# Perceiver layer on one core: a 320-byte gap in front of the transposed token rows in SBUF

## The reference, cut to what matters

```python
x = x + cross_attention(layernorm(x), ctx_2048)   # 4096 context rows + the 256 new ones, one head of 512
x = x + latent_attention(layernorm(x))            # 16 heads, low-rank queries, keys and values, causal, rotary
x = x + moe(layernorm(x))                         # 32 experts, 8 per token in 4 of 8 groups, and a shared expert
```

## Time and profile before

| | us |
|---|---|
| device time, median of 3 runs (lowest, highest) | 524.89 (524.79, 531.13) |
| device time of the profiled execution | 523.41 |
| its span | 521.4 |
| TensorE matmuls, busy in the span | 510.9 (98%) |
| TensorE weight loads | 458.6 (88%) |
| VectorE | 389.1 (75%) |
| ScalarE | 304.4 (58%) |
| GpSimd | 29.4 (6%) |

### The profile page before, as it was taken

The page is one execution under the profiler, slowest core; times in us unless marked ns, Lnnn a source line. Parts: engine busy times, 40 slices in busy tenths (PEclk is TensorE's granted clock), DMA queues, the critical chain, the costliest instruction groups (busy, mean ns, idle before and its releaser), DMA issues.

```text
span 521.4 us, 9657 instructions
## 1 busy us (share of the span) xinstructions
PE 510.9 (98%) x3454; PEld 458.6 (88%) x3454; DVE 389.1 (75%) x616; ACT 304.4 (58%) x470; POOL 29.4 (6%) x48
## 2 busy tenths in 40 slices
PE   8999999999999999989999999999999999999997
PEld 7988888888777998969899999999999999999997
DVE  6777555557889888867787777677776877778675
ACT  5665586655367776664664655546565465645631
POOL 1000000000524113001000000000000000000000
PEclk9999999999999999999999999999999999999999
DMA  8775634545412233333545464655656555464521
GB/s 290 295 232 174 198 123 132 167 162 158 152 35 77 77 97 145 121 123 137 203 142 194 171 224 155 224 182 180 210 163 229 163 200 201 165 233 152 215 72 40
DMA packets 19459, 86.24 MB, mean 165 GB/s; under 512 B 2160, under 2 KB 2416, under 8 KB 19312
## 3 DMA queue, kind: packets, MB, share of 16 engines
q1 hardware_dynamic: 19440, 85.99, 49.0%
HBM read 85.46 MB, written 0.52 MB: 165 GB/s over the span
## 4 chain that ended last, share of the span: by engine, by line
PE 90%; DVE 5%; ACT 2%; issue 1%; DMA 1%; SPq 0%; ACTq 0%; DVEq 0%
PE bank L936 31%; PE bank L429 17%; PE bank L433 16%; PE bank L432 16%; PE bank L437 2%; PE bank L438 1%; PE bank L439 1%; PE bank L573 1%; DVE w_lo L282 1%; PE bank L715 1%; DMA raw<-wq_dram 1%; PE bank L735 1%; PE bank L696 1%; ACT operands L305 1%; DVE xt_lo L330 1%
## 5 line engine op out<-in xcount | busy, mean ns | idle before, releaser
L277 ACT CAST w_hi<-raw 128x768 fp32r<-128x768 f32 (+3 forms) x158 | 159.0, 1041 | 96.6 <-PE bank L936 82.6
L282 DVE TENSOR_TENSOR w_lo<-raw,w_hi 128x1280 fp32r<-128x1280 f32 (+3 forms) x156 | 182.8, 1213 | 13.8 <-ACT w_hi L277 11.7
L429 PE MATMUL bank<-w_hi,operands 128*128 128x512 f32 (+1 forms) x322 | 125.8, 391 | 1.6 <-DVE operands L330 1.0
L433 PE MATMUL bank<-w_hi,operands 128*128 128x512 f32 (+1 forms) x322 | 124.5, 387 | 0.0
L432 PE MATMUL bank<-w_lo,operands 128*128 128x512 f32 (+1 forms) x322 | 123.8, 385 | 0.0
L936 PE MATMUL bank<-xt_hi,w_lo 128*128 128x256 f32 x512 | 105.3, 277 | 0.0
L936 PE MATMUL bank<-xt_hi,w_hi 128*128 128x256 f32 x512 | 105.3, 277 | 0.0
L936 PE MATMUL bank<-xt_lo,w_hi 128*128 128x256 f32 x512 | 105.1, 277 | 0.0
L936 PEld LDWEIGHTS bank<-xt_hi,w_hi 128*128 128x128 f32 x512 | 81.8, 188 | 2.6
L936 PEld LDWEIGHTS bank<-xt_lo,w_hi 128*128 128x128 f32 x512 | 79.8, 188 | 0.0
L936 PEld LDWEIGHTS bank<-xt_hi,w_lo 128*128 128x128 f32 x512 | 79.7, 188 | 0.0
(11 more groups left out here) (182 smaller groups left out, 563.2 us busy)
## 6 DMA issues: line engine op xcount, KB each, us to landing
raw<-w_exp_dram SPq DMA_DIRECT2D x34, 896.0 KB, 4.7
raw<-w_exp_dram SPq DMA_DIRECT2D x34, 640.0 KB, 5.6
raw<-ctx_t_dram SPq DMA_DIRECT2D x16, 512.0 KB, 4.7
raw<-ctx_n_dram SPq DMA_DIRECT2D x16, 512.0 KB, 4.2
raw<-w_mla_dram SPq DMA_DIRECT2D x8, 512.0 KB, 3.5
raw<-w_mla_dram SPq DMA_DIRECT2D x8, 448.0 KB, 3.8
raw<-wq_dram SPq DMA_DIRECT2D x4, 256.0 KB, 5.2
raw<-wk_dram SPq DMA_DIRECT2D x2, 512.0 KB, 7.1
```

What stands on the lines that cost most here:

```text
L277: act.copy(w_hi[:, t.slot, at:at + n], raw[:, t.slot, at:at + n]).then_inc(hi_split[k], 1)
L282: eng.tensor_tensor(w_lo[:, t.slot, at:at + n], raw[:, t.slot, at:at + n], w_hi[:, t.slot, at:at + n].bitcast(F32), ALU.subtract) \
L429: ins = pe.matmul(o, a[0], b[0], start=start, stop=False)
L433: return pe.matmul(o, a[1], b[0], start=False, stop=stop)
```

## The change

One tensor that nothing reads or writes is allocated between `weights` and `xt_hi`, 80 floats (320 bytes) in each partition. `xt_hi`, `xt_lo` and all tensors allocated after them move up by 320 bytes: token rows, `rw_*`, `operands`, `scores`, `probs` and `o_row` from remainder 64 to 384, `rope_w` from 0 to 320. What lies ahead stays: `w_hi` and `w_lo` at 128. No instruction is added, removed or moved.

```diff
         weights = sb("weights", [P, 2, NE])
+        apart = sb("apart", [P, 80])
         xt_hi = sb("xt_hi", [P, NC, T], F32R)
         xt_lo = sb("xt_lo", [P, NC, T], F32R)
```

## The result

The kernel after takes 532.55 us (median of 6, 532.21 to 533.37), the kernel before on the same chip 524.84 (median of 6, 523.39 to 531.13); the ratio is 1.0121 [1.0061, 1.0181]. It is slower by about 1.2%: outside the forecast's direction (521.2, a gain), inside its range of 512 to 535, and within the 2% on which most of its chance lay. The executions of before gather around 524 and around 530.5 us, in changing shares, which is why the intervals here are wide; the profile of before (523.41 us) shows one of the first kind.

A forecast was written before the change was run, and what follows sets the result against it. TensorE, busy 98% of the span, was taken as the bound. Faster matmul paces at the new distances summed to 3.7 us off the profiled 523.4, so 519.7, or 521.2 at the median; range for 8 in 10: 512 to 535.

The forecast's parts named there:

- What bounds the kernel: Whole kernel: TensorE, busy 98% of the span; 90% of the chain that ended last is matmuls; other engines in hand.
- the 120 belongs to equal starts, the best steady pace to unequal ones: Matmuls whose distance changes: 256 columns would run at 113.3 ns and 512 at 226.7; together 3.7 us gained.
- 512 columns: Matmuls of that width were to reach 226.7 ns: scores and context values 0.8 us, new values 0.15 us gained.
- A stumble when the pair changes, which starts far apart should spare: Expert loop: first six gate and up matmuls at 118 ns would reach 113.3; loop gain 0.054 us each, 1.6 us.
- Experts 0 and 1, expert 2, heads: Gains forecast: experts 0 and 1 0.45 us, expert 2 0.3 us, output projection and heads 0.4 us.
- A pair that moved together: Operands with operands, router weights with token rows: distance stays 0, so they were to keep 120 ns.
- A: Rival: weights against token rows or operands settle at expert 2's slower paces; 9.9 us lost, 534.8 us at median; chance 0.23.
- its second variant: Same streams at the paces of equal starts, 120 and 227.5 ns: 8.3 us lost in the loop, 8.6 in all.
- D: Rival: the gap does not land as said; 320 is a multiple of 32, so no padding eats it; given nothing.
- B: Rival: nothing depends on the starts, only on what lies inside 64 bytes; 524.9 us; chance 0.20.
- C: Rival: the floor falls to 109 and 218 ns as far starts remove stalls; 18.3 us gained, 506.6 at median; chance 0.15.
- Its two figures: The Trainium skill's 109.2 and 215.7 ns for matmuls of 256 and 512 columns; gain would be some 20 us.

## Why the prediction was wrong

**What bounds the kernel: right.** The time went nearly whole into TensorE: 9.2 us of span, 9.9 us of busy time, no new wait. "Whatever makes a matmul hold up the next for longer or shorter goes into the time nearly whole" is the loop's arithmetic: 0.287 us a period, 8.31 us between the first and the last.

**The step that failed** is "the 120 belongs to equal starts, the best steady pace to unequal ones", with 256 "as far as it can be" by 512. Equal starts do have 120, but 512 was the wrong measure: it is the bytes that 128 columns take in one partition, and no row of before tells 512 from 256. The runs put 256 in its place: a gap of 256 gives before's paces (5.352 us for 47 starts in both), and equal starts give after's loop to the hundredth of a microsecond (246.50 us). By that measure the change moved token rows from -64 to 0, from the best place for 256 columns to the slowest: 48 matmuls an expert were put at 113.3 and ran at 120.0.

**Not every unequal start is good, either.** The forecast took 113.3 as the floor of all of them. Averages over gate and up (at +32 and +96 over experts 0 and 1 of the gaps of 32 and 480 bytes), and over down or scores, by distance modulo 256:

| distance by 256 | 256 columns, ns | 512 columns, ns |
|---|---|---|
| -96 | 118.6 | not tried |
| -64 | 113.3 or 117.75 | 233.5 |
| -32 | 118.3 | not tried |
| 0 | 120.0 | 226.7 |
| +32 | 116.9 | 233 |
| +64 | 117.7 to 117.9 | 228.8 or 233.0 to 233.8 |
| +96 | 120.0 | 233 |
| 128 | 118.7 | 231 to 232 |

The second pace at +64 was in the forecast's own rows, new values at 233.0 and the down matmuls of the earlier trace rows at 233.8 beside 228.8, and was put down to a stumble. The two columns want different places: 0 is among the slowest for 256 columns and the fastest for 512. With token rows and operands in one block behind the same gap, gate and up at -64 put down at +64; the change paid 0.287 us / 48 = 6 ns on each of an expert's 48 matmuls for a gain that showed in scores and values only.

**512 columns: right in size, nil in the loop.** 226.7 was reached in scores and values (0.34 + 0.23 = 0.57 us gained, 0.8 forecast). In down it came to nothing: 2.747 us before and after, the stumble at the change of pair going from gate and up into down. "A stumble when the pair changes, which starts far apart should spare" fell with it; the operands alone spared it (2.720), and there gate and up fell into 117.75.

**Experts 0 and 1, expert 2, heads: wrong in sign; first projections left out.** They went to 120 from 117.9, 117.75 and, in the first projections, 113.3, each for the reason above; the forecast had gains for the first three and no term for the projections, which were at its floor already. What each stage adds to the 0.63 us by which the loop begins later is read from its first start in both traces: 0.37 stand ahead of the first projection (9.06 and 9.43 us) and need not be of the change, since before itself, run again, begins it at 9.40. The first projections add 0.61; scores take off 0.34, new values 0.13 (227.9 ns, 233.4 before) and context values 0.23; the heads add some 0.26, where the forecast had a gain of 0.4, and experts 0 to 3 the small rest.

**A pair that moved together did not keep its pace.** The router weights against the token rows went from 120 to 116 ns (the last ten starts, 1.20 and 1.16 us). Their slices lie 128 bytes apart, not a multiple of 128 floats as the kernel's section has it of every slice, so two of their four are at distance 128; but the distances are the same in before and after, and so this is another case of one set of distances with more than one pace. It is worth 0.04 us.

**The rivals.** A came, in its second variant: 120 and 227.5, "if it is something shorter than 512 bytes that repeats, so that 256 is as good as 0". It was priced at 8.3 us in the loop (8.31 measured) and 8.6 in all (9.2 measured, 0.37 of it ahead of the first projection), and its period, 8.4 to 8.5, is the 8.500 of the trace. Its own evidence, expert 2 at 117.75, was of something else: the second pace at -64; and of the 32 runs 31 were fast, where the forecast has 30 of 31. D is out, since the paces moved with the gap. B is out: without an instruction changed, starts moved the median from 524 to 532 and back. The Trainium skill, "SBUF — State Buffer", section "Who interferes with whom", calls TensorE's two read ports independent and lets TensorE wait on nobody; it says nothing of starts, and that they could not matter was the prediction's inference from it. Here the pace of the matmuls goes from 113.3 to 120.0 ns with the start of a tensor, so that rule does not price this case. C did not show: no kernel has a steady run of 256-column matmuls over 128 partitions below 113.3. Its two figures from the Trainium skill, "TensorE: Matmul & The Clock Gate", section "Back-to-back issue gap", come by the formula there for an isolated matmul (215.8 for 512 columns, not 215.7), and no run reached them.

**What is shown and what is not.** Shown: the loss is the distance of weights to token rows (moved alone, it is all there), it is a relation (weights moved instead, the same), it repeats with 256 bytes, and at -64 one of two paces holds, which an edit of the matmuls ahead can switch either way. Not shown: what inside the chip repeats with 256 bytes, and what in the matmuls ahead (the moment at which they end, their width, the slot) decides at -64. A theory of banks or of an order of reads would be a story on these numbers.

## What to carry to other kernels

When TensorE is the bound at 98%, where tensors start in SBUF is a parameter of its own: a tensor of 32 bytes added ahead of an operand cost 1.1% here, and it comes unasked with any edit that adds a small buffer. Read paces start to start, by pair and width, note the starts modulo 256 bytes beside them, and before explaining a gain or a loss of 1 or 2% by what an edit was meant to do, give the edit's allocation back by padding and look whether the paces return. Test a placement together with the order of instructions that it will run in, for the pace may depend on what goes before.

## What the runs showed of the hardware that was not expected

- Matmuls of float32r operands with a weight load each run at a pace that depends on the starts of moving and stationary operand, by their difference modulo 256 bytes: 113.3 to 120.0 ns with 256 columns, 226.7 to 233.8 with 512, at a granted clock of 1.00 (2.4 GHz) in the stretch of the loop that was read.
- The sign counts (-64: 113.3, +64: 117.7; with a gap of 128 bytes two stages change places), and the best distance for 256 columns is among the worst for 512 (233.5 at -64).
- At -64 a run of 48 matmuls has 113.3 or 117.75 after its first six or so and keeps it to its end; 512 columns at +64 have two paces as well, 228.8 and 233 to 234. Splitting one matmul ahead of it switches 113.3 to 117.75 in one kernel (531.16 us) and 117.75 to 113.3 in another (523.04 us); in a third the experts take the two in turn, 5.46 and 5.66 us.
